# Attention ends with its last projection; the last group's turning, router and the routing are moved into expert stage 2

## The reference

```
x = x + tanh(g_xattn[0]) * L0_xattn(layernorm(x), ctx)      # one head, stage A of the kernel
x = x + tanh(g_ffn[0])   * L0_ffn(layernorm(x))             # 8 experts, top 2, stage B
x = x + tanh(g_xattn[1]) * L1_xattn(layernorm(x), ctx, ctx) # 16 heads, stage C
x = x + tanh(g_ffn[1])   * L1_ffn(layernorm(x))             # 8 experts, top 2, and one shared, stage D
```

```
scores = sigmoid(h @ W_gate_router)
sel = top_k(scores + expert_bias, 2)
top = take(scores, sel);  top = top / (sum(top) + 1e-20)
expert(h) = (silu(h @ Wg) * (h @ Wu)) @ Wd                  # 96 hidden columns for each expert
out = shared_expert(h) + sum over sel of top * expert(h)
```

## Time and profile before

| | before |
|---|---|
| median of 3 runs | 727.38 us (726.87 to 729.06) |
| profiled execution, its own time | 728.11 us |
| its span, first to last instruction | 726.1 us |
| mean granted TensorE clock | 0.924 |
| PE busy | 635.6 us, 88% |
| DVE busy | 561.4 us, 77% |
| ACT busy | 426.9 us, 59% |
| POOL busy | 103.0 us, 14% |

### The profile page before, as it was taken

One profiled execution on the slowest core, in us unless ns is written; L12 is line 12 of the kernel. 1 busy time (PEld: TensorE's weight loads), 2 busy tenths in 40 slices (PEclk: granted clock), 3 DMA queues, 4 the chain that ended last, 5 costly groups with the idle time before them and its releaser, 6 DMA issues.

```text
span 726.1 us, 12574 instructions
## 1 busy us (share of the span) xinstructions
PE 635.6 (88%) x4078; PEld 498.2 (69%) x4078; DVE 561.4 (77%) x1267; ACT 426.9 (59%) x665; POOL 103.0 (14%) x127
## 2 busy tenths in 40 slices
PE   4765765999999999998599999999997499999996
PEld 3644654787787778776477767777775368888884
DVE  3877766798898889878578787777876588888885
ACT  3342331677777777775287777776675145555553
POOL 3444330020000000000500122022112100000000
PEclk9787565899999999999699999999998599999999
DMA  5323000000000000010244223422300000000000
GB/s 164 110 73 104 23 10 0 1 0 1 2 0 0 0 0 0 0 43 31 70 110 126 80 76 99 128 67 70 104 2 1 1 0 2 16 27 14 14 15 29
DMA packets 23705, 29.34 MB, mean 40 GB/s; under 512 B 3313, under 2 KB 17522, under 8 KB 23666
## 3 DMA queue, kind: packets, MB, share of 16 engines
q1 hardware_dynamic: 23666, 28.84, 13.9%
HBM read 19.99 MB, written 8.85 MB: 40 GB/s over the span
## 4 chain that ended last, share of the span: by engine, by line
PE 67%; DVE 17%; issue 6%; ACT 4%; POOL 2%; DMA 2%; SPq 1%; DVEq 0%; POOLq 0%; ACTq 0%
PE psum L397 13%; PE psum L399 12%; PE psum L398 12%; PE psum L1252 5%; PE psum L1267 3%; DVE c_mx L1423 2%; DVE c_sm L1429 2%; PE psum L1242 2%; PE psum L345 2%; DVE xn L326 2%; PE psum L919 2%; PE psum L1573 2%; PE psum L1243 2%; PE psum L537 2%; POOL rstd L319 1%
## 5 line engine op out<-in xcount | busy, mean ns | idle before, releaser
L397 PE MATMUL psum<-xh,w_hi 128*128 (+1 forms) x248 | 103.0, 415 | 2.2 <-DVE d_hr L1661 1.8
L1364 ACT ACTIVATE c_pt<-psum 77x512 f32<-77x512 f32 x128 | 74.8, 586 | 44.8 <-PE psum L1252 44.7
L398 PE MATMUL psum<-xl,w_hi 128*128 (+1 forms) x248 | 99.4, 401 | 0.0
L399 PE MATMUL psum<-xh,w_lo 128*128 (+1 forms) x248 | 99.2, 400 | 0.0
L869 DVE TENSOR_TENSOR b_hl<-b_hs,b_hh 128x1024 fp32r<-128x1024 f32 x64 | 78.2, 1222 | 15.5 <-ACT b_hh L863 15.5
L985 ACT ACTIVATE b_hr<-psum,b1s 128x512 f32<-128x512 f32 x128 | 81.0, 686 | 15.6 <-PE psum L399 15.5
L1045 DVE TENSOR_TENSOR b_hs<-b_hr,psum 128x1024 f32<-128x1024 f32 x64 | 77.8, 1215 | 15.3 <-ACT b_hr L985 13.8
L863 ACT ACTIVATE b_hh<-b_hs 128x1024 fp32r<-128x1024 f32 x64 | 67.9, 1061 | 33.1 <-PE psum L399 33.0
L1252 PE MATMUL psum<-ident,c_pf 128*77 128x128 f32 x512 | 74.4, 282 | 0.1
L1252 PEld LDWEIGHTS psum<-ident,c_pf 128*77 128x77 f32 x512 | 58.1, 149 | 14.4 <-issue 10.6
L1423 DVE TENSOR_REDUCE c_mx<-psum 128x8 f32<-128x616 f32 x64 | 50.9, 796 | 18.9 <-PE psum L1243 18.7
(11 more groups left out here) (209 smaller groups left out, 1271.9 us busy)
## 6 DMA issues: line engine op xcount, KB each, us to landing
w_hi<-c_q_spread SPq DMA_DIRECT2D x24, 256.0 KB
stage<-in_weights SPq DMA_DIRECT2D x8, 576.0 KB, 5.1
c_q_spread<-w_hi SPq DMA_DIRECT2D x7, 512.0 KB, 3.5
ctxg<-in_ctxT SPq DMA_DIRECT2D x16, 156.0 KB, 4.3
c_k_spread<-w_lo SPq DMA_DIRECT2D x8, 312.0 KB, 2.2
x_all<-in_x SPq DMA_DIRECT2D x8, 256.0 KB, 2.8
out_dram<-x_all SPq DMA_DIRECT2D x8, 256.0 KB, 2.3
c_kb<-c_k_spread SPq DMA_DIRECT2D x48, 39.0 KB
```

The costliest lines, as they stand in the source:

```text
L397: pe.matmul(o, wh, h, start=start, stop=False)
L398: pe.matmul(o, wh, l, start=False, stop=False)
L399: return pe.matmul(o, wl, h, start=False, stop=stop)
L1364: a_.activation(pt[:, q % NC4, :], bank[2 + q % 2][0:S2, :], ACT.Copy).then_inc(pt_done, 1)
```

## The change

- Stage C loses its step 10 (`drain=2`). Group 7's turning of `xn`, its splitting, its router product, the turning of that and the copy of its logits move into stage D's first group (chunks 1 to 5), with bank 7 in place of bank 6 as their PSUM bank.
- PE no longer waits for the splitting of group 7 ahead of stage D. It waits for the last scores, the last probabilities and the last division, and for the residual of group 7 (`c_res`) ahead of the first `down`.
- The routing done in stage C is that of 20 tiles (groups 0 to 4, 160 elements), and begins in step 8: its parts are spread over the odd slots of step 8 and slots 0 to 4 of step 9. Its buffers lie in `above`.
- The small DVE setup of stage D and the placing of group 0 (`dve_gate`) move to slot 5 of stage C's step 9.
- The routing of the other 12 tiles (96 elements) takes place in stage D's second and third group, one part a chunk. Its exponential on ACT comes in chunk 6 of the first group, between two uses of `Silu`, and ahead of ACT's copy of group 1's weights, which PE's turning of them (moved from chunk 2 to chunk 6) feeds.
- Stage D runs by `pipeline3`: the same ten steps, the first four of them written out instead of two.

More of the change, by code:

```diff
@@ L95, in pipeline, with groups, pipeline4 @@
     step(None, None, Group(None, NG - 1))
-def pipeline4(eng, step):
+def pipeline3(eng, step):
+    def groups(i, c):
+        return [Group(i, c - k) if c - k >= 0 and (i is not None or c - k < NG) else None for k in range(3)]
+    for c in range(4):
[5 more added lines that the diff above has]
+        step(*groups(None, c))
+def pipeline4(eng, step, drain=3):
     def groups(i, c):
@@ L106, in pipeline4 @@
         step(*groups(i, 5))
-    for c in range(NG, NG + 3):
+    for c in range(NG, NG + drain):
         step(*groups(None, c))
@@ L339, in pool_norm, with place, pe_transpose @@
                                 ALU.mult).then_inc(self.xn_ready, 1)
-            def pe_transpose(self, pe, g):
+            def place(self, other):
+                return self.bank if other is None else other
+            def pe_transpose(self, pe, g, other=None):
                 xo = self.bufs[4]
@@ L734, in first, with first_part, second_part @@
                     self.values = logits[:, self.tiles, :]
[L735 to L742, removed]
-                self.pick(v, self.values, r1["m"], rt["first"][:])
+                self.pick(v, self.values, r1["m"], rt["first"][:])
+            def plus_one(self, v):
[9 more added lines that the diff above has]
+                                             eb1[:].unsqueeze(1).broadcast_to([P, self.n, E]), ALU.add))
+            def first_part(self, v, k):
+                self.pick_part(v, k, self.values, self.r1["m"], self.rt["first"][:])
+            def second_part(self, v, k):
+                self.pick_part(v, k, self.rt["wt"][:], self.r1["m2"], self.rt["second"][:])
             def second(self, v):
@@ L780, in split, with chosen, normed, gated @@
                     link(v, v.tensor_tensor(rt["wt"][:], rt["pick"][:], rt["tmp"][:], ALU.add))
[L781 to L786, removed]
-                    link(v, v.tensor_tensor(rt["wt"][:], rt["tmp"][:], bc(r1["w1"]), ALU.mult))
+                self.gated(v)
+            def chosen(self, v):
+                rt, r1, link = self.rt, self.r1, self.link
+                link(v, v.tensor_tensor(rt["pick"][:], rt["first"][:], rt["second"][:], ALU.add))
+                link(v, v.tensor_tensor(rt["tmp"][:], rt["pick"][:], rt["sig"][:], ALU.mult))
+                link(v, v.tensor_reduce(r1["d"], rt["tmp"][:], AX.X, ALU.add))
+            def normed(self, v):
+                rt, r1, link = self.rt, self.r1, self.link
+                link(v, v.tensor_scalar(r1["m"], r1["d"], EPS_ROUTE, None, ALU.add))
+                link(v, v.reciprocal(r1["w1"], r1["m"]))
+                link(v, v.tensor_tensor(rt["wt"][:], rt["tmp"][:], self.bc(r1["w1"]), ALU.mult))
+            def gated(self, v):
+                rt, link = self.rt, self.link
                 gate = tg[:, 2 + self.layer:3 + self.layer]
@@ L1693, in step @@
                         xd.dve_residual(v, t, MISC)
-            pipeline(v, step)
+            pipeline3(v, step)
         dve_parts.append(dve_d)
```

61 lines of the change are left out of this document (32 added, 29 removed).

## The result

The median of nine runs is 723.42 us (719.83 to 726.72), that of the kernel before in as many runs 729.21 us (726.87 to 730.91). The ratio is 0.992, with a 95% interval of 0.9897 to 0.9943. 721.5 had been forecast, against 727.38 for the kernel before: a ratio of 0.992 too. In time that is 5.8 us less, where 5.9 had been forecast.

A forecast was written before the change was run, and what follows sets the result against it. PE, busy 88% of the span, was taken as the bound, recoverable where it waits on the serial chain before stage D. Terms -8.2 + 1.2 + 0.8 + 0.3 = -5.9 gave 721.5 us, 8-in-10 range 717.8 to 725.0.

The forecast's parts named there:

- The place, 8.2 us earlier: End of stage C: PE goes straight from last projection to stage D's place, at 569.1 instead of 577.3 us.
- Step 8: Stage C's attention loop, set by DVE: routing instructions exceed free slot time, making all that follows 2.8 us later; bounds 1.4 to 4.8.
- Step 9 behind `xl`: Stage C: nine routing instructions between `xl` and the output's copy lie whole on the path, 2.95 us; bounds 2.2 to 3.7.
- the five instructions: Slot 15 of step 8, slots 0 and 1 of step 9: 1.8 us of routing fits the pause before `xl`.
- Stage D's first group, +1.2: From place: later chunk 2 +0.6, product, logits transposes and `xl` stall +1.9, old routing stalls gone -1.3; sum +1.2 us.
- the stall at `xn`: Stage D's first group: PE waits for POOL's `xn` for 0.1 to 0.5 us; 0.1 with the clock as before.
- The table of ACT, +0.8: Stage D, chunk 6: two more table loads make `st` 0.8 us late for PE, late `Silu` hidden; bounds 0 to 2.9.
- Routing in groups 2 and 3, +0.3: Stage D: new routing exceeds DVE's free time, losing 1.3 us (bounds 0 to 2.8); an old stall of 0.98 goes.
- signs of being wrong: Projection ending past 571, PE waiting over 2 us at a hand-off, or stage D's first three groups over 4 us longer.
- slower: Rival, chance 0.06: the moved chain stalls PE 2.6 us at each of four hand-offs in stage D's first group; 729.7 us.
- Step 8 hides the routing: Rival, chance 0.15: PE's waits in stage C's loop hide part of the lag; 719.3 us, or 718.0.
- ACT's two switches reach PE: Rival, chance 0.15: both table loads and the exponential in stage D delay PE whole, 2.9 us instead of 0.8; 723.6 us.

The follow-up runs named there:

- e3_double_step8: Changed kernel with every routing instruction of slots 1 to 13 of step 8 run twice; first to last maximum of step 8 28.58 us, against 23.84.
- e2_step9: Changed kernel with `chosen` and `normed` moved to slot 1 of step 9, `gated` and stage D's setup to slot 7; `xl` to last projection 4.74 us, against 8.27.
- e5_after_copy: Changed kernel with `second_part(1)` moved from slot 0 to slot 1 of step 9, behind DVE's output copy; step 8 to end 191.96 us, against 193.57.
- e1_no_switch: Changed kernel with the last 12 tiles' exponential replaced by a plain copy, so no table switches in stage D; step 8 to end 191.39 us, against 193.57.
- e6_handoffs: Changed kernel with group 1's placing in chunk 0, group 7's transposes in chunk 2, `st` copied before the exponential; step 8 to end 191.45 us, against 193.57.
- e8_all_silu: e7_all plus e5_after_copy's order, with the last 12 tiles' sigmoid as silu(x) / x, needing no other table; ratio to kernel before 0.9797, median 713.73 us.
- e7_all: Changed kernel with the orders of e2_step9 and e6_handoffs together, same work; ratio to the kernel before 0.9857, median 717.97 us.

## Why the prediction was right

**The place, 8.2 us earlier: 8.26 measured** (41.86 against 50.12 us after the first maximum). Step 8 cost 2.48 where 2.8 were given, and slot by slot it is as reckoned: up to the maximum of slot 4 it came 0.66 later (0.7 given), then 0.10 (0.2), 0, 0.64 (0.7), 0.70 (0.7) and 0.39 (0.45). e3_double_step8 shows that nothing there is hidden. The bound of 4.8 for this term takes in the two instructions of slot 15, behind the last maximum; the slots listed hold 4.1. Step 9 behind `xl` cost 2.63 (8.27 against 5.64) where 2.95 were given, for ten instructions where there are nine. They delay the copy by 2.92; the rest was covered by a wait of 0.29 for `lt_s` that PE had before. And 0.84 that wasn't in the sum came ahead of `xl`, where the five instructions were said to fit into a pause: L728 was held, and the output's copy, which stood behind it on DVE, came late for PE. e2_step9 and e5_after_copy take these two away one by one. That 8.2 was hit so closely is in part luck: two terms 0.3 too high each stand against the missing 0.84.

**Stage D's first group, +1.2: +1.56 measured** (593.13 - 573.19 = 19.94 against 18.4). The chain from the residual to `xn` took 5.80 us (573.51 to 579.31), 5.8 was given. But the stall at `xn` was given as 0.1 to 0.4 and is 1.27: the clock was back by 575.33, in the first chunk and not from the second on, and the sooner PE is there, the longer it waits for POOL's unchanged chain. With it chunk 2 starts 6.54 us after the place, 0.9 later than before, where 0.6 was given. The stall at `xl` is 0.65, 0.8 was given.

**The table of ACT, +0.8: 1.8 measured** (e1_no_switch). The spreading came 1.3 late for `st`, not 0.8. And the step that said the `Silu` is hidden was wrong by 0.5, the tail in groups 2 and 3; e6_handoffs shows why it is a near thing, since the stall ahead of it was its cover. The drain of ScalarE: Activation LUTs in the Trainium skill doesn't show: in e6_handoffs the exponential ends at 589.02, the load runs from 589.03 to 590.31, and `Silu` starts at 590.32. A switch there holds ACT for 1.3 us, not 2.66, so the page's drain isn't why the term was too low.

**Routing in groups 2 and 3, +0.3: -1.2 measured.** This is the term that was most mis-sized (the prediction counts from 0 and calls them groups 1 and 2). The old routing's stalls went, as reckoned (1.26 in the second group, 18.37 against the 17.11 of e1_no_switch; 0.98 were given). But the new routing, for which 1.3 of loss stood in the sum, costs nothing: with all of it in place these groups take 17.1 us in e1_no_switch and e8_all_silu, like every later group. The price of the instructions was right (24 rows of 6.3 us and the links between them, 7.2 in all); what was too small is the free time set against it, 0.4 us a chunk from the busy share. Rows of steady work, from the kernel before, and one chunk with routing from the changed kernel:

```profile
626.01 0.69 DVE L1661 TENSOR_TENSOR d_hr<-d_hr,psum 128x512 f32<-128x512 f32 x1
627.10 0.69 DVE L869 TENSOR_TENSOR d_hl<-d_hs,d_hh 128x512 fp32r<-128x512 f32 x1 [0.40 <-ACT d_hh L863]
627.71 0.68 DVE L1668 TENSOR_TENSOR d_hs<-d_hr,psum 128x512 f32<-128x512 f32 x1
628.33 0.69 DVE L1661 TENSOR_TENSOR d_hr<-d_hr,psum 128x512 f32<-128x512 f32 x1
```

```profile
607.81 0.69 DVE L1742 TENSOR_TENSOR d_hr<-d_hr,psum 128x512 f32<-128x512 f32 x1
608.41 0.68 DVE L908 TENSOR_TENSOR d_hl<-d_hs,d_hh 128x512 fp32r<-128x512 f32 x1
609.01 0.68 DVE L1749 TENSOR_TENSOR d_hs<-d_hr,psum 128x512 f32<-128x512 f32 x1
609.61 0.25 DVE L731 TENSOR_TENSOR route_first<-route_tmp,r_c 128x96 f32<-128x96 f32 x1
```

Back to back the three instructions of a chunk start 0.60 us apart, 1.8 us of a chunk's 2.44, so that 0.64 is free and not 0.4; and with routing between the chunks the wait for `d_hh` is gone. An estimate from these rows: 14 chunks have 9.0 us free, less 1.7 for two residuals and two places, which leaves 7.2, just what the routing takes.

**The sum.** From group 2's first product (593.13, before 595.70) to the fourth group's first spreading it is 36.87 us before, 37.47 in the changed kernel and 35.69 in e1_no_switch, so the switches are +1.78 of this and the rest -1.18. Together -8.26 + 1.56 + 1.78 - 1.18 + 0.77 = -5.33 us, where 0.77 is groups 4 to 7 and the last group, all but 0.01 of it clock. Against the forecast of -5.9 that is a routing term 1.5 too high, a table term 1.0 too low, 0.4 in the first group and a clock of 0.8 that nobody forecast: the mechanisms of the main term are right, the closeness of the total is luck.

Of the signs of being wrong one came true by its letter: the projection ends at 573.4, past 571. But this trace was 4.1 us late before step 8; without that it is 569.3, where 569.1 had been given. Of the rivals, "slower" needed 2 us at each hand-off: there were 1.27, 0.65, 0 and 1.12. "Step 8 hides the routing" is out by e3_double_step8, and "ACT's two switches reach PE" (2.9) holds in part, with 1.8.

## What to carry to other kernels

A serial chain at a stage's end, in which the busiest engine only waits, is worth moving into the next stage's first work even if its pieces then stall that engine a little: 14 us of hand-offs became 3 us of stalls. Then look at each piece's place in each queue, since the same nine instructions cost 2.6 us or nothing by the slot they stood in. And price work put on a second engine by what its instructions take back to back, not by its busy share in steady work: there rows that overlap when they are packed stand apart, and short waits vanish once there is other work at that point.

## What the runs showed of the hardware

A DVE tensor-tensor that reads two tiles in SBUF was held while POOL ran a tensor-tensor over SBUF, and ended 0.17 to 0.18 us after POOL's: 1.28 and 0.93 us instead of 0.31 (changed kernel, e5_after_copy). In e3_double_step8 it is another instruction that meets POOL's, L726, with 0.92 us instead of 0.33, and it too ends 0.18 after. DVE's copy out of PSUM at the same time ran on, and so did a reduction of one tile in SBUF (L725 in e3_double_step8, 0.31 us). SBUF — State Buffer in the Trainium skill (SBUF: two separate sides) says that the two engines share a port pair which one holds for a whole instruction, for DVE with two SBUF inputs against a GpSimd instruction that reads SBUF; these traces agree. One place doesn't show it: in the kernel before, L708 took its usual 0.39 us from 567.12 on, inside the 1.04 us of POOL's 128x4 tensor-tensor (L319, from 566.83). The cause was read from the times alone: no run took POOL's instruction away.

TensorE's clock differed between executions of one order: the last turning of the output took 0.63 us in e2_step9 and 1.09 in e7_all, which were equal up to there, and the last matmuls of the kernel ran at full clock before and at half in the changed kernel. In these traces that moved up to 1.2 us in the last group and 0.9 between `xl` and the last projection. What decides it wasn't found.
